# Two-layer graph network on one core: dense stage first, base and turned output in one PSUM bank, statistics of two chunks at once

## What is computed

```python
h = relu(layernorm(x))
x_l, x_r = h @ W_l + b_l, h @ W_r + b_r              # 4 heads of 32
m = leaky_relu(x_l[s] + x_r[d], 0.2)                 # edges and self loops
e = einsum('ehc,hc->eh', m, att); e = exp(e - segment_max(e, d)[d])
alpha = e / segment_sum(e, d)[d]
x = x + segment_sum(alpha * x_l[s], d) + bias        # layer 1
h = relu(layernorm(x))
Wij = (ssp(edge_attr @ Wf1 + bf1) @ Wf2 + bf2) * edge_weight
agg = segment_sum((h @ W_in)[src] * Wij, dst)
x = x + ssp(agg @ Wo1 + bo1) @ Wo2 + bo2             # layer 2
```

## Time and profile before

| | us |
|---|---|
| median of 3 runs | 3281.08 |
| lowest and highest | 3272.99, 3284.18 |
| profiled execution, its own time | 3285.26 |
| span in its profile | 3283.3 |
| busy: PE, DVE, ACT, POOL | 2703.7, 2662.2, 2292.9, 1898.8 |

### The profile page before, as it was taken

How to read it: one execution, slowest core, us unless ns; L and a number is a source line. 1 busy time by engine, 2 the same in 40 slices (tenths; PEclk the granted TensorE clock), 3 DMA queues, 4 the chain that set the end, 5 groups by cost and what they waited for, 6 DMA issues and landing times.

```text
span 3283.3 us, 58511 instructions
## 1 busy us (share of the span) xinstructions
PE 2703.7 (82%) x16380; PEld 1783.9 (54%) x16380; DVE 2662.2 (81%) x6911; ACT 2292.9 (70%) x4901; POOL 1898.8 (58%) x1583
## 2 busy tenths in 40 slices
PE   2999988888888888888868877788778878758887
PEld 2666664444444444444435555555555555547776
...
DMA packets 266476, 546.16 MB, mean 166 GB/s; under 512 B 82627, under 2 KB 159069, under 8 KB 228671
## 3 DMA queue, kind: packets, MB, share of 16 engines
...
...
## 4 chain that ended last, share of the span: by engine, by line
PE 25%; issue 20%; DVE 16%; POOL 15%; ACT 14%; DMA 7%; SPq 1%; POOLq 0%; ACTq 0%; DVEq 0%
POOL sum_dram L588 9%; ACT d_n L990 6%; POOL x_dram L576 6%; PE bank L1177 4%; PE bank L1359 3%; PE bank L1256 3%; ACT a_nd L1009 2%; PE bank L1261 2%; DMA sum_dram<-b_sum,b_at 2%; DVE f_ssp_out L941 2%; PE bank L1211 2%; DVE a_max L790 2%; ACT turned L987 2%; DMA x_dram<-b_xo,sidx 2%; ACT f_ln_out L1162 2%
## 5 line engine op out<-in xcount | busy, mean ns | idle before, releaser
L588 POOL DMA_INDIRECT sum_dram<-b_sum,b_at x392 | 651.0, 1661 | 135.1 <-issue 104.6
L541 POOL DMA_INDIRECT a_xs<-in_x,index x392 | 390.2, 995 | 353.5 <-ACT a_ns L1009 171.7
L546 POOL DMA_INDIRECT a_xd<-in_x,index x392 | 403.1, 1028 | 124.2 <-issue 101.7
L576 POOL DMA_INDIRECT x_dram<-b_xo,sidx x294 | 346.3, 1178 | 103.2 <-issue 91.3
L1328 PE MATMUL bank<-b_rows,b_same 128*128 128x128 bf16 x4704 | 339.8, 243 | 0.0
L1328 PEld LDWEIGHTS bank<-b_rows,b_same 128*128 128x128 bf16 x4704 | 325.0, 111 | 0.0
L990 ACT ACTIVATE d_n<-d_x,stat_d_shift,stat_d_rstd 128x128 f32<-128x128 f32 x686 | 283.7, 486 | 0.2 <-DVE stat_d_shift L624 0.2
L1359 PE MATMUL bank<-wo,f_ssp_out 128*128 128x128 f32 x1568 | 226.5, 288 | 56.7 <-DVE f_ssp_out L941 51.9
L553 POOL DMA_INDIRECT x_dram<-a_xo,index x98 | 101.7, 1038 | 286.0 <-DVE a_xo L807 263.7
L1211 PE MATMUL bank<-wl,turned 128*128 128x128 f32 x1568 | 228.9, 289 | 38.2 <-ACT turned L987 27.5
L941 DVE SCALAR_TENSOR_TENSOR f_ssp_out<-bank,cols,f_ln_out 128x512 f32<-128x512 f32 x196 | 147.1, 750 | 123.3 <-ACT f_ln_out L1162 102.4
...
## 6 DMA issues: line engine op xcount, KB each, us to landing
d_x<-in_x SPq DMA_DIRECT2D x49, 1024.0 KB
x_dram<-d_x SPq DMA_DIRECT2D x49, 1024.0 KB, 4.9
d_x<-x_dram SPq DMA_DIRECT2D x49, 1024.0 KB, 12.0
out<-d_x SPq DMA_DIRECT2D x49, 1024.0 KB, 8.2
sum_dram<-zero SPq DMA_DIRECT2D x48, 1024.0 KB
d_n<-sum_dram SPq DMA_DIRECT2D x25, 1024.0 KB, 9.9
...
```

The lines of the kernel that those rows point to most:

```text
L541: pool.indirect_dma_start(a_xs[i][:, j * F:(j + 1) * F], None, x, column(t, j)).then_inc(gathered[t % GSEM], 16)
L546: pool.indirect_dma_start(a_xd[i][:, j * F:(j + 1) * F], None, x, column(t, TILES + j)).then_inc(gathered[t % GSEM], 16)
L576: pool.indirect_dma_start(x1_dram, bass.IndirectOffsetOnAxis(ap=sidx[s][:, j:j + 1], axis=0), b_xo[s][:, j * F:(j + 1) * F], None, bounds_ ...
L588: pool.indirect_dma_start(sum_dram, bass.IndirectOffsetOnAxis(ap=b_at[s][:, j:j + 1], axis=0), b_sum[s][:, j * F:(j + 1) * F], None, compu ...
```

## The change

- **Start.** SP's first issue is the first node load, followed by the seven loads that the output bias needs, three more node loads, and then the other weights. The edge lists, the edge weights and the setup stores are issued by POOL. On DVE the dense stage comes first; output bias, lists, edge weights and index columns stand behind the steps of groups 0, 1, 2 and 3 (`beside`). PE makes the bias's matmul after the second quad's transposes, and turns the lists after group 2.
- **Gathers.** Half-chunks of two transfers. The first 24 chunks are issued one source or target set per dense group. Later POOL first scatters chunk t, which waits for `early_ready`, and then issues up to the larger of an even share and all of chunk t+5.
- **Base and output in one bank.** `a_base` is gone. PE writes bias, `a_hd` by `wl` of chunk t−2 and `a_o` by the identity (a matmul in place of the transpose) into bank 6 or 7 by turns, and DVE's `a_x1` adds the target rows themselves, whose ring slot becomes free two steps later. `a_hd` has three buffers.
- **Statistics.** `sums_a` runs two chunks ahead; in odd steps the small operations and the shift are done for two chunks, 16 columns at once.
- `EARLY` becomes a pair, (1, 1), which changes nothing by itself.

```diff
-EARLY = 1
+EARLY = (1, 1)
...
-        a_hd = sb("a_hd", [P, C])
+        a_hd = [sb(f"a_hd{i}", [P, C]) for i in range(3)]
...
-        a_base = two("a_base", [P, TILES * F])
...
-        LATE = 16 * (TILES - EARLY)
+        def early(s):
+            return EARLY[s] * F
+
+        def late(s):
+
+            return 16 * (TILES - EARLY[1 - s])
...
-            def const(tile, a):
-                sp.dma_start(tile, a).then_inc(load_const, 16)
-
-            for tile, a in ((wl, W_l), (wr, W_r), (win, W_in), (wf2, Wf2), (wo1, Wo1), (wo2, Wo2)):
+            def const(tile, a, loaded=load_const):
+                sp.dma_start(tile, a).then_inc(loaded, 16)
+
...
+            load(0, 0)
+            const(wl[:, :], W_l, load_first)
+            const(wo2[:, :], Wo2, load_first)
+            const(cols[:, 5:6], bo1.rearrange("(f o) -> f o", o=1), load_first)
+            for n, a in enumerate((b_l, bias, bo2)):
+                const(rows3[:, n * F:(n + 1) * F], a.rearrange("(a f) -> a f", a=1).broadcast_to([3, F]), load_first)
+            const(bo2_all[:, :], bo2.rearrange("(a f) -> a f", a=1).broadcast_to([P, F]), load_first)
+            for g in range(1, RX):
+                load(g, g)
+
+            for tile, a in ((wr, W_r), (win, W_in), (wf2, Wf2), (wo1, Wo1)):
                 const(tile[:, :], a)
...
+            pool.memset(ident[:, :], 0.0)
+            pool.memset(ones3[:, :], 1.0)
             pool.memset(raw[:, 0, :], 0)
             pool.memset(raw[:, 1, :], SKIP)
             pool.memset(raw[:, 2:4, :], -1)
             pool.memset(weight_f[:, :], 0.0).then_inc(pool_setup, 1)
+            pool.wait_ge(pool_setup, 1)
+            pool.affine_select(out=ident[:, :], in_=ident[:, :], compare_op=ALU.not_equal, fill=1.0, base=0,
+                               pattern=[[-1, P]], channel_multiplier=1).then_inc(pool_setup, 1)
...
+            by_chunk(0, 0, FULL, src[0:FULL * C])
+            part(0, FULL, 0, src[FULL * C:E])
...
+            flat = attr_dram.rearrange("e r -> (e r)")
+            pool.dma_start(flat[0:E * RBF].rearrange("(a b) -> a b", a=400),
+                           edge_attr.rearrange("e r -> (e r)").rearrange("(a b) -> a b", a=400)).then_inc(store_setup, 16)
...
-            def gathers(t):
...
+            def gather_src(t, h):
+                if h == 0:
+                    if t >= GSEM:
+                        pool.wait_ge(gathered[t % GSEM], 128 * (t // GSEM))
+                        pool.sem_inc(pool_step, 1)
+                    if t >= DEPTH:
+                        pool.wait_ge(norm_src, t - DEPTH + 1)
+                        pool.sem_inc(pool_step, 1)
+                for j in (2 * h, 2 * h + 1):
+                    pool.indirect_dma_start(a_xs[t % DEPTH][:, j * F:(j + 1) * F], None, x, column(t, j)).then_inc(gathered[t % GSEM], 16)
+
+            def gather_dst(t, h):
+                if h == 0 and t >= DEPTH:
-                    pool.wait_ge(norm_src, t - DEPTH + 1)
+                    pool.wait_ge(x1_ready, t - DEPTH + 1)
                     pool.sem_inc(pool_step, 1)
...
             for t in range(DEPTH):
-                gathers(t)
+                for n, gather in enumerate((gather_src, gather_dst)):
+                    pool.wait_ge(d_x1_ready, QUADS * min(RX + 1 + 2 * t + n, NG))
+                    pool.sem_inc(pool_step, 1)
+                    for h in range(2):
+                        gather(t, h)
-            for t in range(NC + 2):
-                if t + DEPTH < NC:
-                    gathers(t + DEPTH)
-                if t >= 2:
-                    early_scatters(t - 2)
+
+            rest = [(gather, t, h) for t in range(DEPTH, NC) for gather in (gather_src, gather_dst) for h in range(2)]
+            done = 0
+            for t in range(NC):
+                early_scatters(t)
+                until = min(len(rest), max(-(-len(rest) * (t + 1) // NC), 4 * (t + 6 - DEPTH)))
+                for gather, g, h in rest[done:until]:
+                    gather(g, h)
+                done = max(done, until)
...
             sums_d(0, 0, 0, 0)
             sums_d(0, 0, 0, 1)
             statistics_d(0, 0)
+            beside = (output_bias, edge_lists, edge_weights, index_columns)
             for g in range(RX):
                 step_d(g, g, 0, back=g > 0, back2=g > 1)
+                beside[g]()
             with dve.Fori(1, 1 + ROUNDS) as m:
...
             def sums_a(t):
-                st = stat_e[t % 2]
+                st = stat_e[t // 2 % 2]
+                n = t % 2 * 2 * TILES
                 dve.wait_ge(gathered[t % GSEM], 128 * (t // GSEM + 1))
                 for j in range(TILES):
-                    dve.bn_stats(st["six"][:, j, :], a_xs[t % DEPTH][:, j * F:(j + 1) * F])
+                    dve.bn_stats(st["six"][:, n + j, :], a_xs[t % DEPTH][:, j * F:(j + 1) * F])
                 for j in range(TILES):
-                    last = dve.bn_stats(st["six"][:, TILES + j, :], a_xd[t % DEPTH][:, j * F:(j + 1) * F])
-                last.then_inc(six, 1)
+                    last = dve.bn_stats(st["six"][:, n + TILES + j, :], a_xd[t % DEPTH][:, j * F:(j + 1) * F])
+                if t % 2:
+                    last.then_inc(six, 1)
 
             def step_a(t):
                 s = t % 2
                 o = 1 - s
-                front = t < NC
-                ahead = t + 1 < NC
+                pair = (t + 1) // 2
+                paired = t % 2 == 1 and t + 1 < NC
                 mid = 1 <= t <= NC
                 back = t >= 2
                 if mid:
...
                     dve.wait_ge(out_turned, t - 1)
                     if t >= 4:
                         dve.wait_ge(end_stored[s], 16 * ((t - 4) // 2 + 1))
-                    dve.tensor_tensor(a_x1[s][:, :], bank[7][:, :], a_base[s][:, :], ALU.add).then_inc(x1_ready, 1)
-                if ahead:
-                    sums_a(t + 1)
+                    dve.tensor_tensor(a_x1[s][:, :], bank[6 + s][:, :], a_xd[(t - 2) % DEPTH][:, :], ALU.add).then_inc(x1_ready, 1)
+                if t + 2 < NC:
+                    sums_a(t + 2)
                 if back:
                     dve.wait_ge(x1_ready, t - 1)
                     if t >= 4:
-                        dve.wait_ge(early_scattered[s], 16 * EARLY * ((t - 4) // 2 + 1))
-                    dve.tensor_tensor(a_xo[s][:, 0:EARLY * F], a_x1[s][:, 0:EARLY * F], bo_row[:, 0:EARLY * F], ALU.add).then_inc(early_ready, 1)
-                if front:
-                    dve.wait_ge(base_mm, t + 1)
-                    dve.tensor_tensor(a_base[s][:, :], bank[6][:, :], a_xd[t % DEPTH][:, :], ALU.add).then_inc(base_ready, 1)
-                if ahead:
-                    statistics(dve, stat_e[o], 2 * TILES, six, sumdif, sq, var, t + 1, t + 2)
+                        dve.wait_ge(early_scattered[s], 16 * EARLY[s] * ((t - 4) // 2 + 1))
+                    dve.tensor_tensor(a_xo[s][:, 0:early(s)], a_x1[s][:, 0:early(s)], bo_row[:, 0:early(s)], ALU.add).then_inc(early_ready, 1)
+                if paired:
+                    statistics(dve, stat_e[pair % 2], 4 * TILES, six, sumdif, sq, var, pair, pair + 1)
                 if mid:
 
                     dve.wait_ge(exp_decay, t)
                     dve.scalar_tensor_tensor(out=a_dec[:, :], in0=a_decay[:, :], scalar=1.0, in1=a_keep[o][:, :],
                                              op0=ALU.min, op1=ALU.mult).then_inc(decay, 1)
-                if ahead:
-                    shifts(dve, stat_e[o], 2 * TILES, rstd, shift, t + 2)
+                if paired:
+                    shifts(dve, stat_e[pair % 2], 4 * TILES, rstd, shift, pair + 1)
                 if mid:
                     dve.wait_ge(exp_score, t)
                     dve.wait_ge(decay, t)
...
-                if ahead:
-                    inverse_deviation(act, stat_e[o], 2 * TILES, var, log_var, rstd, t + 2)
+                if ahead and t % 2:
+                    inverse_deviation(act, stat_e[(t + 1) // 2 % 2], 4 * TILES, var, log_var, rstd, (t + 1) // 2 + 1)
...
+            def output_bias():
+                pe.wait_ge(weights_ready, 1)
+                pe.matmul(bank[7][:, 0:F], bo1_all[:, :], wo2[:, :], start=True, stop=True).then_inc(index_turned, 1)
...
                 d_turn(g, slot, 0)
                 for q in range(1, QUADS):
                     d_turn(g, slot, q)
+                    if first and q == 1:
+                        output_bias()
                     d_multiply(g, q - 1)
...
                 if t >= 2:
-                    pe.wait_ge(att_out, t - 1)
-                    if t >= 3:
-                        pe.wait_ge(x1_ready, t - 2)
-                    turn_tiles(bank[7], a_o[s]).then_inc(out_turned, 1)
+                    c = t - 2
+                    to = bank[6 + s]
+                    if c >= 2:
+                        pe.wait_ge(x1_ready, c - 1)
+                    pe.matmul(to[:, :], ones3[:, 0:P], bias3[:, :, :].rearrange("k j f -> k (j f)"), start=True, stop=False)
```

(21 more changed lines are left out.)

286 lines of the change are left out of this document (136 added, 150 removed).

## The result

The changed kernel takes 3322.5 us (median of 4, 3317.2 to 3331.0) against 3281.8 us for the one before (median of 4): a ratio of 1.0132, 95% interval 1.0103 to 1.0160. Measured again beside the kernel before on two chips it gave 1.0142 (1.0109 to 1.0175) and 1.0145 (1.0123 to 1.0166). It is slower by 1.3 to 1.4%. The prediction's 3279.7 us missed by 43 us, and its range ended at 3315.

A forecast was written before the change was run, and what follows sets the result against it. It took ACT to bound the dense stage and DVE to be busiest (92%) in attention, with PE waiting for ACT; −35.3 (start) − 8.3 (steady steps) + 42.2 (late gathers) = −1.4 us gave 3279.7 us, range 3230 to 3315.

The forecast's parts named there:

- Start: Setup and dense stage: first node load issued first, −46.8 us, less 5.4 and 6.1 for the setup moved inside, −35.3 us.
- rival 4: Dense stage: the edge lists come late and DVE stalls up to 14 us; 3294 us, chance 0.13.
- The other insertions: Dense stage: edge lists, edge weights and index columns put after groups 1, 2 and 3, 8.6 us partly hidden, +6.1 us.
- Steady steps: Attention stage: 12.20 us with statistics, 11.48 without, mean 11.84 against 11.94; about −8 us over 83 steps.
- closed chain: Attention step: PE's turn to a_x, to a_all's end, through ACT back to PE's turn; 12.20 or 11.48 us.
- Rival 3: Attention stage: the clock keeps falling, +1.8 us every second step, +75 us over 83 steps; 3354 us, chance 0.13.
- Gathers behind a wait: Late attention steps, t = 78 to 92: POOL gathers chunk t+5 behind a wait, 14.75 us a step, +42 us.
- loop: Late attention steps: signal 0.1, POOL's scatter and eight gathers 10.0, landing 2.8, DVE's statistics and a_xo 1.84; 14.75 us.
- rival 1: Late attention steps: POOL is not late, the gathers arrive in time; 3236 us, chance 0.13.
- rival 2: Attention stage: PE's passes slip into its idle time, a_x need not wait, each step sheds 0.96 us; 3208 us, chance 0.06.
- rival 5: Late attention steps: gathers land at the slow end, 15.65 us a step; 3293 us, chance 0.06.

## Why the prediction missed

- **Start.** Forecast −35.3, measured −31.6 in the trace and −33.7 and −32.2 us in the two versions that hold it alone. DVE began at 5.79 us (5.7), the first addition came at 26.6, 20.8 us later instead of 13.6 before: 7.2 us for what had been put at 5.4. The output bias took its 6.7 us and cost 5.2 of them, about as forecast; the other 2.0 are DVE's first two columns of `d_n`, which took 2.58 instead of 0.60 us, and about as long in all seven traces with this start on the first kind of chip. Why stays open. DVE waited for no list: rival 4 did not happen. The other insertions cost 7.8 us from the first addition on (410.0 : 417.8), not 6.1.
- **Steady steps.** 12.22 and 11.52 us where 12.20 and 11.48 were forecast, DVE waiting 1.21 us for PE: the closed chain was right, and so was the judgement that nearly all that DVE sheds turns into waiting. Yet the first 77 steps took 4.9 us more, not 8 less. The difference of −0.07 a step gives −5; the rest, +10, lies in the first steps, before the rhythm sets in, and in five steps of 13.07 to 14.32 us in which the clock fell. The forecast had put these falls at nothing.
- **Clock.** 0.99 instead of 0.93. Rival 3's mechanism exists, and costs 1.55 us (13.07 instead of 11.52; PE's rows below: turn, bias and base passes at the low level, the output passes nearly spared), but it comes in one step of some 15, not in every second. The Trainium skill (TensorE: Matmul & The Clock Gate, Part 4: PE-mode transpose) says that a transpose doesn't count as PE-busy the same way. The falls in 5 of 38 cases instead of 46 of 50 (The clock, above) are in line with it.

```profile
1197.90 1.04 PE L1209 MATMUL bank<-ident,a_nd 128*128 128x128 f32 x4 [1.83 <-ACT a_nd L1041]
1198.88 0.60 PE L1290 MATMUL bank<-bias,ones 3*128 3x512 bf16 x1
1199.41 2.08 PE L1292 MATMUL bank<-wl,a_hd 128*128 128x128 f32 x8
1201.28 1.14 PE L1295 MATMUL bank<-ident,a_o 128*128 128x128 f32 x8
```

- **Gathers behind a wait: the step that failed.** The loop is the one that was described, and its place is right; its size was taken at 14.75 us for 15 steps (+42), and it is 16.19 us for 17 (+72). The longer round makes some 25 us of the difference, the two extra steps some 6. By parts, for the round of 15.91 us shown above: from the end of a_xo to POOL's next issue 0.91 us, where 0.1 had been put for a signal; from the scatter to the last gather's start 10.69 us (10.7 to 10.8 and 11.2 by turns, 12.0 once), where eight times 1.25 gave 10.0, because some issues take longer (the next one starts 1.58 us after the scatter at 1507.50 and 1.57 us after the gather at 1514.12); landing 2.47 us against 2.8; statistics and a_xo 1.84 as forecast. The two extra steps come from the even share: at t = 76 and 77 it no longer reaches beyond chunk t+5 either (296 x 76 / 98 gives 230 half-chunks issued by t = 75, and the first 58 chunks of the rest are 232), so these gathers too are wanted one step after the wait. The signal could have been read from before: its POOL scatter at 1407.76 was released by this a_xo, which ended 0.87 us earlier:

```profile
1406.61 0.28 DVE L807 TENSOR_TENSOR a_xo<-a_x,bo_row 128x128 f32<-128x128 f32 x1
```

- **Rivals 1, 2 and 5.** POOL was late (against 1), PE's passes didn't slip into its idle time by themselves (against 2; they do when the program puts them there), and landing wasn't slow (against 5): the excess came from issue and signal.
